# The router's eight columns ride in a half-filled product of the experts' first layer

## The reference, cut to what matters

```
shared = _mlp(x, w_fc_sh, w_proj_sh)          # square(relu(x @ wfc)) @ wproj
logits = xf.astype(jnp.float32) @ router_w.T  # 8 experts
scores = jax.nn.sigmoid(logits)
_, idx = jax.lax.top_k(scores + balance_bias, K)   # K = 2
tw = jnp.take_along_axis(scores, idx, axis=-1)
tw = tw / (tw.sum(-1, keepdims=True) + 1e-20)
combine = (jax.nn.one_hot(idx, E, dtype=tw.dtype) * tw[..., None]).sum(1)
h = jnp.square(jax.nn.relu(jnp.einsum('nc,ech->neh', xf, w1)))
y = jnp.einsum('neh,ehc->nec', h, w2)
routed = jnp.einsum('nec,ne->nc', y, combine)
```

## Time and profile before

| what | us |
|---|---|
| median of three runs | 5201.05 (5198.89 to 5211.17) |
| the profiled execution's own time | 5215.72 |
| its span, first to last instruction | 5214.0 |
| TensorE busy, products | 4763.4 (91%) |
| TensorE busy, weight loads | 4490.0 (86%) |
| VectorE busy | 3365.6 (65%) |
| ScalarE busy | 2270.1 (44%) |
| GpSimd busy | 561.3 (11%) |
| mean granted TensorE clock | 0.953 |

### The profile page before, as it was taken

The page is one execution under the profiler, slowest core; times in us unless marked ns, Lnnn a source line. Parts: engine busy times, 40 slices in busy tenths (PEclk is TensorE's granted clock), DMA queues, the critical chain, the costliest instruction groups (busy, mean ns, idle before and its releaser), DMA issues. The chain is left out here.

```text
span 5214.0 us, 92414 instructions
## 1 busy us (share of the span) xinstructions
PE 4763.4 (91%) x31272; PEld 4490.0 (86%) x31272; DVE 3365.6 (65%) x9549; ACT 2270.1 (44%) x6372; POOL 561.3 (11%) x529
## 2 busy tenths in 40 slices
PE   4775799899899899989989999998999799999999
PEld 4765699899899889989988988998998699999999
DVE  4555566667666756766666676676666566666666
ACT  2443555555455545555555545555553122222221
POOL 1122000000000000000000000000000333333332
PEclk9887899999999999999999999999999899999999
DMA  6452000000000000000000000000000100000000
GB/s 138 99 123 62 6 1 1 1 20 1 1 20 1 1 2 20 1 1 20 1 1 20 1 1 1 20 1 1 10 1 3 42 16 18 18 18 16 16 18 18
DMA packets 65157, 99.50 MB, mean 19 GB/s; under 512 B 3763, under 2 KB 60674, under 8 KB 61120
## 3 DMA queue, kind: packets, MB, share of 16 engines
q1 hardware_dynamic: 61312, 90.31, 6.9%
q0 software_dynamic: 944, 2.42, 0.3%
q10 hardware_dynamic: 2560, 2.36, 0.2%
HBM read 65.88 MB, written 29.20 MB: 18 GB/s over the span
## 5 line engine op out<-in xcount | busy, mean ns | idle before, releaser
L643 ACT ACTIVATE att_prob<-att_s,att_npeak 99x198 f32<-99x198 f32 x1536 | 638.8, 422 | 1229.6 <-DVE att_npeak L816 1186.5
L816 DVE TENSOR_REDUCE att_npeak<-att_s 99x2 f32<-99x396 f32 x768 | 436.2, 568 | 901.1 <-PE att_s L988 899.0
L971 PE MATMUL att_o<-att_probT,att_vx 99*96 99x198 f32 (+1 forms) x3072 | 686.1, 346 | 1.3 <-ACT att_probT L633 1.3
L988 PE MATMUL att_s<-att_kx,att_qx 96*99 96x198 f32 (+1 forms) x3072 | 659.2, 337 | 3.6 <-DVE att_xres L782 2.7
L1351 PE MATMUL ffn_y<-ffn_down,ffn_hidden 128*128 128x192 f32 x3564 | 637.4, 329 | 6.8 <-DVE ffn_acc L1262 4.9
L1351 PEld LDWEIGHTS ffn_y<-ffn_down,ffn_hidden 128*128 128x128 f32 x3564 | 590.0, 191 | 29.4 <-DVE ffn_acc L1262 27.5
L971 PEld LDWEIGHTS att_o<-att_probT,att_vx 99*96 99x96 f32 (+1 forms) x3072 | 511.6, 182 | 42.3 <-issue 32.7
L988 PEld LDWEIGHTS att_s<-att_kx,att_qx 96*99 96x99 f32 (+1 forms) x3072 | 518.6, 169 | 19.0 <-issue 4.6
L806 DVE TENSOR_SCALAR att_prob<-att_prob,att_total 99x198 f32<-99x198 f32 x1536 | 459.1, 342 | 26.9
L1132 POOL TENSOR_TENSOR ffn_hidden<-ffn_relu 128x384 f32<-128x384 f32 x462 | 378.7, 826 | 764.9 <-ACT ffn_relu L1159 457.2
L1159 ACT ACTIVATE ffn_relu<-ffn_h 128x384 f32<-128x384 f32 x231 | 113.0, 489 | 705.7 <-PE ffn_h L1340 705.5
(11 more groups left out here) (208 smaller groups left out, 9611.7 us busy)
## 6 DMA issues: line engine op xcount, KB each, us to landing
tok_pixels<-in_x SPq DMA_DIRECT2D x24, 1568.0 KB
ffn_hid<-hidden SPq DMA_DIRECT2D x34, 288.0 KB, 2.9
att_xres<-hidden SPq DMA_DIRECT2D x8, 1188.0 KB
hidden<-att_xres SPq DMA_DIRECT2D x8, 1188.0 KB
out_hidden<-ffn_acc SPq DMA_DIRECT2D x33, 288.0 KB, 2.3
hidden<-tok_rows SPq DMA_DIRECT2D x8, 1176.0 KB
att_oT<-in_L_attn_qkv_w ACTq DMA_DIRECT2D x1, 1536.0 KB, 11.1
tok_posb<-in_L_tok_pos_embedding POOLq DMA_DIRECT2D x1, 1176.0 KB, 42.4
```

The source lines that it names most:

```text
L643: ins = nc.scalar.activation(prob[:, i % 2, h, :], s_bank[i % 2][0:HALF, h * NTOK:(h + 1) * NTOK], ACT.Exp, bias=npeak[:, i % 2, h:h + 1], ...
L816: nc.vector.tensor_reduce(npeak[:, i % 2, :], s_bank[i % 2][0:HALF, 0:2 * NTOK].rearrange("p (h k) -> p h k", h=2), AX.X, ALU.max, negate= ...
L971: ins = nc.tensor.matmul(o_bank[j % 2][0:M, 0:NTOK], vx[:, p % 2, 2 * b + k, v0:v0 + M], probT[:, j % 2, k * NTOK:(k + 1) * NTOK], start=( ...
L988: ins = nc.tensor.matmul(s_bank[i % 2][0:HALF, h * NTOK:(h + 1) * NTOK], qx[0:K, p % 2, head, q0:q0 + HALF], kx[0:K, p % 2, head, b * NTOK ...
```

## The change

The router's 8 columns are computed as rows 64 to 71 of the half chunk 13, whose product has 72 output rows where it had 64. It gets a sixth product (low part by low part), which the router had. ScalarE takes exp(-x) of these 8 rows for all 384 tokens into a new buffer `odds`, whose other 120 partitions were cleared at the start. Three transposes on TensorE turn it so that the tokens stand on the partitions, and VectorE adds 1 while it reads them from the accumulator bank. The 18 narrow products go. In TensorE's order the wait for xT_made moves to the first chunk, and `route` comes after the second down product.

```
@@ gpsimd, ahead of the other clearings
+                nc.gpsimd.memset(odds[:, :], 0.0).then_inc(odds_cleared, 1)
@@ scalar
                 def exponentials(k):
-                    act.wait_ge(routed, k + 1)
-                    nc.scalar.activation(expo[:, :, :], r_bank[:, 0:TB * EXPERTS].rearrange("p (t e) -> p t e", t=TB),
-                                         ACT.Exp, scale=-1.0).then_inc(expo_made, 1)
+                    act.wait_ge(up_done, k * HT + UPS.index(13) + 1)
+                    if not isinstance(k, int):
+                        act.wait_ge(routed, k)
+                    nc.scalar.activation(odds[0:EXPERTS, :], h_bank[1][64:64 + EXPERTS, 0:BT], ACT.Exp, scale=-1.0
+                                         ).then_inc(expo_made, 1)
...
                     high(it + 1)
-                    exponentials(it + 1)
                     for k, numbers in enumerate(AFTER):
                         relus(it + 1, numbers)
+                        if k == 0:
+                            exponentials(it + 1)
@@ vector, route, part 0
-                        dve.wait_ge(expo_made, it + 1)
-                        step(nc.vector.tensor_scalar(expo[:, :, :], expo[:, :, :], 1.0, None, ALU.add))
+                        dve.wait_ge(routed, it + 1)
+                        step(nc.vector.tensor_scalar(expo[:, :, :], view(r_bank[:, :], [[128, TB], [1, EXPERTS]]), 1.0, None, ALU.add))
@@ tensor
                 def route(k):
-                    pe.wait_ge(xT_made, k + 1)
+                    pe.wait_ge(expo_made, k + 1)
                     for t in range(TB):
-                        cols, wc = slice(t * 128, (t + 1) * 128), slice(HID, HID + EXPERTS)
-                        o = r_bank[:, t * EXPERTS:(t + 1) * EXPERTS]
-                        parts = ((x0h, w0h), (x0l, w0h), (x0h, w0l), (x0l, w0l), (x1, w1h), (x1, w1l))
-                        for i, (a, b) in enumerate(parts):
-                            ins = nc.tensor.matmul(o, a[:, cols], b[:, wc], start=(i == 0), stop=(i == len(parts) - 1))
+                        cols = slice(t * 128, (t + 1) * 128)
+                        ins = nc.tensor.transpose(r_bank[:, cols], odds[:, cols], ident[:, :])
                     ins.then_inc(routed, 1)
@@ tensor, ups
-                        rows = 64 if j == 13 else 128
+                        rows = 64 + EXPERTS if j == 13 else 128
                         wc = slice(128 * j, 128 * j + rows)
+                        if n == 0:
+                            pe.wait_ge(xT_made, k + 1)
...
-                        parts = ((w0h, x0h), (w0h, x0l), (w0l, x0h), (w1h, x1), (w1l, x1))
+                        parts = ((w0h, x0h), (w0h, x0l), (w0l, x0h), (w1h, x1), (w1l, x1)) + (((w0l, x0l),) if j == 13 else ())
@@ tensor, the order
+                ups(0, (0, 1))
                 route(0)
-                ups(0, range(HT))
+                ups(0, range(2, HT))
                 with pe.Fori(0, BLOCKS - 1) as it:
                     turn(it + 1)
-                    down_(it, 0)
-                    route(it + 1)
-                    ups(it + 1, AFTER[0])
-                    for k in range(1, MLPS):
+                    for k in range(MLPS):
                         down_(it, k)
+                        if k == 1:
+                            route(it + 1)
                         ups(it + 1, AFTER[k])
```

More of the change, by code:

```diff
@@ L1036, in experts_stage @@
         relu = m.sb("relu", [128, 4, BT])
+        odds = m.sb("odds", [128, BT])
         bb, ranks = m.sb("bb", [128, EXPERTS]), m.sb("ranks", [128, EXPERTS])
@@ L1055, in experts_stage @@
         down_done, summed, acc_out = m.sem("down_done"), m.sem("summed"), [m.sem(f"acc_out{i}") for i in range(2)]
-        down_cleared = m.sem("down_cleared")
+        down_cleared, odds_cleared = m.sem("down_cleared"), m.sem("odds_cleared")
         h_tiles = hidden1.rearrange("b n d -> (b n) d").rearrange("(t p) d -> p t d", p=128)
@@ L1163, in _ @@
                 high(0)
+                act.wait_ge(odds_cleared, 1)
                 exponentials(0)
```

## The result

The changed kernel takes 5148.52 us (median of 4 runs, 5142.06 to 5154.77), the kernel before 5202.67 (median of 4, 5198.89 to 5211.17). The ratio is 0.9894, with a 95% interval of 0.9876 to 0.9911: 54 us less. The forecast was 5141.7, with a range of 5133 to 5167.

What follows compares the result with a forecast made beforehand. TensorE was taken as the only full engine in the expert loop. Loop passes -47.5, first block +3.5 and clock falls -15.4 sum to -59.4 us, from a median of 5201.05 to 5141.7 us; range 5133 to 5167.

Steps and rivals of the forecast that it cites:

- 18 products removed, 2.03 us: Loop block, TensorE: dropping the router's 18 narrow products saves 2.03 us a block, all on the path.
- The sixth product, 72 rows at no cost: Half chunk: one more 384-column product adds 0.175 us a block; 72 output rows instead of 64 add nothing.
- Three transposes, 0.33: Loop block, TensorE: three added transposes at 0.11 us each cost 0.33 us.
- the change of kind, 0 to 0.14: Product groups following another kind of instruction: +0.04 behind a down product; none behind the transposes, bounds 0.14 either way.
- The wait for the transposed input: TensorE's wait for VectorE moves from the router to the first chunk, its length the same 0.45 us.
- The new wait is nothing: Transposes waiting for ScalarE's exponential: no wait, some 0.15 us to spare, bounds 0 and 0.3 us.
- T+3.6: Forecast end of ScalarE's exponential, in us after T, the start of the block's first chunk.
- First block +3.5: Block outside the loop: late chunk +2.0 us, plus one clock fall of 1.54; together +3.5, bounds +1.5 and +5.
- 32 passes of 1.485: Expert loop: each block net 1.485 us shorter, so 32 passes give -47.5 us.
- The falls go, -15.4: Clock drops behind the router in 10 of 32 passes vanish with the narrow products: -15.4 us, bounds -15.4 and 0.
- Rival 3: Transposes make the clock fall in every loop block: +5.3 us, or +14.9 with a wait, 5216 us; chance 0.04.

Runs made afterwards that it cites:

- w12_filler: Changed kernel plus 12 unused products of 384 columns between first down product and first chunk of each loop pass: 5214.34 us, ratio 1.002.
- early_transposes: Changed kernel with its three transposes right behind the half chunk, ahead of the second down product: 5203.16 us, ratio 0.9993.
- n18_shifted: Changed kernel plus 18 unused narrow products at the router's old place and five wide products behind the three transposes: 5260.13 us, ratio 1.0102.
- b_route_moved: Kernel before with its 18 narrow router products moved behind the second down product, exponential behind the first relu: 5194.31 us, ratio 0.9979.

## Why the prediction was right

- **18 products removed, 2.03 us**: right. Putting them back cost 2.02.
- **The sixth product, 72 rows at no cost**: right; starts 0.17 apart in the timeline after.
- **Three transposes, 0.33, and the change of kind, 0 to 0.14**: right in sum. From the second down product's start to the next chunk's are 2.20 us (4261.20 to 4263.40), where the down product alone takes 1.81: 0.39. The chunk behind takes 0.96 instead of 1.01, so 0.34 is left.
- **The wait for the transposed input, "its length the same"**: off by 0.09 us a block. I moved the wait as if it stayed the same wait; now an instruction of its own carries it, and TensorE starts later behind it (3.01 us from the transposes, where it was 2.92). That it is not the wider product shows in `w12_filler`: its first product is as wide, carries the wait itself, and starts 2.92 us behind the transposes. Small gains elsewhere bring the sum to the measured 1.44 instead of 1.485: the first chunk takes 0.98 (4259.18 to 4260.16), 0.01 more than before and not 0.04, and the half chunk grew from 0.88 to 1.04 us, by 0.16 and not 0.175.
- **The new wait is nothing**: right. ScalarE was done at T+3.54 where I had T+3.6, and `early_transposes` shows what the cover is worth, 1.63 us a block. The Trainium skill's 1.38 us of draining behind a table load (ScalarE: Activation LUTs, What ACT_TABLE_LOAD costs) does not show here: the load ends at 4262.22 and the exponential starts at 4262.24.
- **First block +3.5**: the step was under-sized, +5.2. Its part up to the late chunk was right (11.80 us from the first chunk, 9.82 from the first router product before: +1.98, forecast +2.0). Behind it the same work at the lower clock took 15.49 us where it took 13.57, so 1.9 and not 1.5, and the weights landed 1.3 us later against the stage's start. That last is no effect of the change that I can show: over the thirteen profiles the start of the weights' conversion varies from 17.3 to 20.6 us behind the stage's start; the changed kernel's is the latest.
- **32 passes of 1.485**: the first pass does not fit. It gained 0.3 us, since it starts at a lower clock than before. The prediction's price for the low clock ended with the first block.
- **The falls go, -15.4**: right in sign and size, and the reason only in part. I put them down to the narrow products. `n18_shifted` shows that these bring falls in up to every second pass, `b_route_moved` that without the old neighbours they brought none, in one run. The change did two things: it took the products away, and it moved the router's work behind the second down product. With the products moved and not removed the falls stayed away at one block length, 33.75 us; whether the move alone is enough at others isn't shown. Which of the old neighbours matters, the transposes or the wait of 0.45 us, stays open: no run separated them.
- **Rival 3, a fall in every block through transposes**: fell. The Trainium skill (TensorE: Matmul & The Clock Gate, Part 4: PE-mode transpose) says that transposes don't count as busy as products do. These runs don't bear out what I feared from it: 18 in a row, 2 us, had no fall behind them in any pass at three block lengths, where narrow products at the same place had 3, 2 and 15.
- **The median** came out 6.8 us above the forecast: 4.2 us lie in the stage (55.2 in place of 59.4): 1.7 in the first block, 1.2 in the first pass, 1.3 in the 0.04 us that each of the other blocks is longer than forecast. The rest is within the scatter of the runs.

## What to carry to other kernels

Few columns don't make a cheap product: with 8 columns it took 0.113 us from start to start here, where a transpose with 128 took 0.11, each with a weight load of its own. Count the starts in the timeline, and let such columns ride in a product that is under-filled. When a result goes round through another engine, write down when it is back and put enough work of the waiting engine in between; the same instructions in an order with 1.8 us less cover cost the whole gain. And an engine that is busy for 98% still may have places where it waits: a dummy that costs less than its own length finds them; moving VectorE's work away from that place, with the first block's routing spread, gave another 29 us (5148.5 to 5119.5).

## What the runs showed of the hardware

- The clock's falls changed in number with the length of the whole loop pass: 3, 2 or 15 of 32 passes with the same 18 products at the same place, in blocks of 34.16, 34.25 and 35.1 us. With 18 transposes there, in blocks of 34.95 us, none. One profile with few falls says little about a variant a half microsecond longer.
- Three transposes of 128 columns behind a down product took 0.25 us to the start of the next product (4263.15 to 4263.40), less than three times the 0.11 of the earlier trace rows; 0.14 was lost ahead of them instead.
- The same semaphore wait costs 0.09 us more where an instruction of its own carries it than on the product itself: 3.01 us from the block's first transpose in the changed kernel, 2.92 in `w12_filler`, with the same kind of product behind it, in every block looked at.
